# A graph layer on one core: normalised rows and transposed exponentials moved from VectorE to ScalarE

## What is computed

```
xn = layernorm(x)
x  = x + segment_sum(edge_weight * xn[dst], src) + mix(xn)
x  = x + moe(layernorm(x))            # 8 experts, top 2

mix(f):  Q, K, V = f @ W_q + b_q, f @ W_k + b_k, f @ W_v + b_v
         sm  = softmax(K, axis = nodes)
         lam = sm.T @ V                # 256 x 256
         bn  = batchnorm(lam) * gamma + beta
         return Q @ bn
```

## Time and profile before

| | |
|---|---|
| median of 3 runs | 2375.08 us (2373.32 to 2385.05) |
| profiled execution | 2391.07 us, its span 2389.3 us, mean granted clock of TensorE 0.949 |
| PE busy | 2092.6 us, 88% of the span |
| PE weight loads busy | 1786.0 us, 75% |
| DVE busy | 1496.7 us, 63% |
| ACT busy | 1148.2 us, 48% |
| POOL busy | 1420.8 us, 59% |

### The profile page before, as it was taken

The page is one execution under the profiler, slowest core; times in us unless marked ns, Lnnn a source line. Parts: engine busy times, 40 slices in busy tenths (PEclk is TensorE's granted clock), DMA queues, the critical chain, the costliest instruction groups (busy, mean ns, idle before and its releaser), DMA issues. The chain is left out here.

```text
span 2389.3 us, 36271 instructions
## 1 busy us (share of the span) xinstructions
PE 2092.6 (88%) x11864; PEld 1786.0 (75%) x11864; DVE 1496.7 (63%) x2726; ACT 1148.2 (48%) x3466; POOL 1420.8 (59%) x1282
## 2 busy tenths in 40 slices
PE   5798589998999899989998999899999964888885
PEld 3476477987888789878987888789889963666664
DVE  7895387758775777587758775877467766010112
ACT  4520154555456545554565455545566640333332
POOL 1001667667776776677667776776666621666663
PEclk9998899999999999999999999999999986999996
DMA  7523722232233222322232223222233321555666
GB/s 248 164 71 120 246 89 80 84 92 81 77 87 93 79 79 84 91 82 80 84 91 80 80 87 91 78 83 83 86 112 116 116 86 43 180 182 183 209 210 226
DMA packets 157570, 270.85 MB, mean 113 GB/s; under 512 B 28310, under 2 KB 105125, under 8 KB 157385
## 3 DMA queue, kind: packets, MB, share of 16 engines
q0 software_dynamic: 59584, 161.78, 22.7%
q1 hardware_dynamic: 62796, 72.81, 9.3%
q10 hardware_dynamic: 35004, 33.93, 4.8%
HBM read 223.61 MB, written 45.77 MB: 113 GB/s over the span
## 5 line engine op out<-in xcount | busy, mean ns | idle before, releaser
L1154 POOL DMA_INDIRECT edge_G<-xn_scratch,edge_row_i x1029 | 1165.7, 1133 | 488.2 <-issue 262.2
L1254 ACT ACTIVATE edge_weighted<-edge_hots,bins_scale 128x128 f32<-128x128 bf16 x2401 | 738.7, 391 | 52.3 <-DVE edge_row_hots L1311 52.3
L1221 PE MATMUL edge_op<-edge_win,edge_A 128*128 128x256 f32 x2744 | 663.6, 385 | 60.5 <-issue 43.4
L1221 PEld LDWEIGHTS edge_op<-edge_win,edge_A 128*128 128x128 f32 x2744 | 523.7, 192 | 148.6 <-issue 55.3
L1245 ACT COPY edge_A<-edge_ap 128x512 f32<-128x512 f32 x343 | 200.8, 585 | 734.9 <-PE edge_ap L1204 530.2
L1217 PE MATMUL edge_op<-edge_G,edge_weighted 128*128 128x256 f32 x2058 | 511.0, 384 | 25.8 <-DVE all_xn L1324 21.4
L1306 DVE TENSOR_TENSOR edge_hots<-bins_iota128b,bins_recb 128x1024 bf16<-128x1024 bf16 x343 | 237.1, 691 | 367.8 <-PE edge_ap L1204 272.0
L1217 PEld LDWEIGHTS edge_op<-edge_G,edge_weighted 128*128 128x128 f32 x2058 | 364.7, 191 | 71.8 <-DVE all_xn L1324 25.6
L1204 PEld LDWEIGHTS edge_ap<-edge_weighted,edge_row_hots 128*128 128x128 f32 x2744 | 359.1, 194 | 54.0 <-DMA edge_win<-xn_scratch 13.6
L1204 PE MATMUL edge_ap<-edge_weighted,edge_row_hots 128*128 128x128 f32 x2744 | 371.5, 279 | 15.8 <-DMA edge_win<-xn_scratch 13.2
L1311 DVE TENSOR_TENSOR edge_row_hots<-all_iota,bins_recd 128x512 f32<-128x512 f32 x343 | 238.5, 695 | 0.0
(11 more groups left out here) (291 smaller groups left out, 1849.3 us busy)
## 6 DMA issues: line engine op xcount, KB each, us to landing
exp_w1x<-in_w ACTq DMA_DIRECT2D x105, 256.0 KB
edge_G<-xn_scratch,edge_row_i POOLq DMA_INDIRECT x1029
exp_ys<-ys_scratch SPq DMA_DIRECT2D x12, 1024.0 KB
ln_xin<-in_x SPq DMA_DIRECT2D x12, 512.0 KB, 5.7
xn_scratch<-ln_xnb ACTq DMA_DIRECT2D x12, 512.0 KB, 6.8
xnT_scratch<-ln_xT SPq DMA_DIRECT2D x12, 512.0 KB, 7.0
mix_xg<-xn_scratch SPq DMA_DIRECT2D x12, 512.0 KB, 3.9
mix_ek<-xnT_scratch SPq DMA_DIRECT2D x12, 512.0 KB, 4.8
```

Of the source, the lines that this page charges most:

```text
L1154: pool.indirect_dma_start(out=G[:, t % AHEAD, i, :], out_offset=None, in_=xn_dram, in_offset=bass.IndirectOffsetOnAxis(ap=row_i[:, q % 2, ...
L1221: last = nc.tensor.matmul(op[j][:, :], A[:, j, i, :], win[:, q % 2 * DN + i, :], start=False, stop=i == DN - 1)
L1254: last = nc.scalar.activation(weighted[:, t % 2, i, :], hots[:, t % 2, i // 2, :, i % 2], ACT.Copy, scale=scale[:, b, i:i + 1])
```

## The change

Two edits. In the norm stage VectorE normalises one row of tiles of a group and ScalarE the other three. In the mix stage the copy of the transposed exponentials, `evac`, goes from VectorE to ScalarE with its waits: unit 0 between the exponentials of groups 0 and 1, and unit u+1 at the head of ScalarE's step u, in front of the exponentials of a later group and of ScalarE's share of the binning. VectorE keeps its other work in its old order.

```diff
-    DVE_ROWS = 2
+    DVE_ROWS = 1
...
+                def evac(u):
+                    act.wait_ge(p_turned, u + 1)
+                    if u >= PB:
+                        act.wait_ge(p_used, u - PB + 1)
+                    rows = tiles_of(u)
+                    r, w = rows[0], len(rows) * D
+                    nc.scalar.copy(pt[:r, u % PB, 0:w], kp[u % 2][:r, 0:w]).then_inc(p_out, 1)
+
                 exps(0)
+                evac(0)
                 exps(1)
                 for u in range(U):
+                    if u + 1 < U:
+                        evac(u + 1)
                     if u % 2 == 1 and u // 2 + 2 <= NG:
                         exps(u // 2 + 2)
                     for n in IN_SUMS[u]:
...
-                def evac(u):
-                    dve.wait_ge(p_turned, u + 1)
-                    if u >= PB:
-                        dve.wait_ge(p_used, u - PB + 1)
-                    rows = tiles_of(u)
-                    r, w = rows[0], len(rows) * D
-                    nc.vector.tensor_copy(pt[:r, u % PB, 0:w], kp[u % 2][:r, 0:w]).then_inc(p_out, 1)
-
-                evac(0)
                 bins.dve_relate(dve)
                 for u in range(U):
-                    if u + 1 < U:
-                        evac(u + 1)
                     for n in IN_SUMS[u]:
                         bins.dve_share(dve, 0, n)
```

## The result

The changed kernel took 2369.32 us (median of 20 runs, 2363.16 to 2375.15), the kernel before beside it 2374.57 (20 runs, 2368.21 to 2385.05). The ratio is 0.9979, with an interval of 0.9969 to 0.9988: 5 us faster, by its interval 2.9 to 7.4 us. The profiled execution took 2373.04 us, its span 2371.3, against 2391.07 and 2389.3 before. One run in this document, of the cut kernel with the order fixed (297.36 us), was in a slower state of the chip and is left out of its median.

The account below looks back on a forecast made before the run. TensorE, full beside VectorE in the main mix sums (128.2 to 187 us), was taken as the bound there. Norm stage -0.1 and mix sums -0.7 gave -0.8 us: from 2375.08 to 2374.3 us, range 2366 to 2381.

Parts of the forecast that it names:

- The case of a small gain of 0 to 4 us: Whole kernel: the forecast itself, likeliest time 2374.3 us; chance 0.73.
- the step for the copies ahead of the restart: Mix stage: four copies of 0.60 us leave VectorE's queue before the first slot matrix, so TensorE restarts 2.4 us earlier.
- The slow clock: Mix stage: TensorE's longer wait before its restart costs 0 to 1.7 us more at lower clock; 1.7 taken.
- rival (2): Mix sums: VectorE is what really bounds them, so 18 us go, giving 2357 us; chance 0.04.
- Behind the scaled sums: End of mix stage: the chain of dependent steps to 212 us and the last pass run as now.
- the first meeting: Norm stage, group 5: VectorE's shift starts 0.77 us before GpSimd's subtraction, so the 3 us stall goes.
- The two delays of the first groups: Norm stage: by group 5, +0.65 us on VectorE's shift and +1.5 us on ScalarE's cast, hence on GpSimd's subtraction.
- Rival (1): Norm stage: the stall stays, the stage ends 3.0 us later, kernel 2.3 us slower at 2377.4; chance 0.2.
- the term that was mis-sized: Norm stage: one-hot comparisons may meet GpSimd's second subtraction, at most one instruction's wait, inside VectorE's slack.
- part 1: Norm stage: stall gone (-2.05 us) against four longer ScalarE normalisations of 0.49 us each, -0.1 us at its end.
- Busy times: Both early stages: VectorE about 22 us less busy, ScalarE about 22 us more, by mean durations.
- Rival (3): Mix stage: copies queue behind the exponentials on ScalarE, TensorE gives 17 us back, 2391 us; chance 0.03.

Follow-up runs that it names:

- cut kernel with the order fixed: Kernel before, ended behind the mix stage, with GpSimd's two subtractions made to wait for VectorE's rows of groups 5 and 7: 293.09 us.
- third chip: Chip where four whole kernels were run against the kernel before (2241.71 us); the changed kernel took 2238.95 us there, ratio 0.9989.
- cut kernel before: Kernel before without its edge, routing and expert stages, storing x after the mix stage: 298.35 us.
- kernel with the useless matmuls: Changed kernel, ended behind the mix stage, with 44 unused matmuls in TensorE's wait for the first slot matrix: 294.14 us.
- cut kernels with two rows: Two kernels ended behind the mix stage, VectorE keeping two rows: the kernel before (298.35 us) and one with only the copies moved to ScalarE (295.00 us).
- cut pair: Kernel before and changed kernel, both ended behind the mix stage: 298.35 and 294.86 us, difference -3.5 us (-5.6 to -1.7).
- the kernel with the order fixed: Whole kernel before, nothing moved, GpSimd's two subtractions waiting for VectorE's rows of groups 5 and 7: 2238.51 us, ratio 0.9979.
- cut one with only the row: Kernel before, ended behind the mix stage, with one row moved to ScalarE and the copies left on VectorE: 296.19 us against 298.35.

## Why the prediction held, and where it was off

*Sign and size.* Forecast -0.8 us, 2374.3; measured 5.2 us less, 2369.3, inside the range of 2366 to 2381. The case of a small gain of 0 to 4 us was the right one of the four, its size too small. On the third chip the same change gave 2.8 us, with an interval that reaches zero. The range was made wide for the wandering of the medians, so a number inside it says little about the mechanisms; those are gone through one by one.

*Mix stage: the step for the copies ahead of the restart.* Right. 4 x 0.60 = 2.4 us was the term. In VectorE's order of time the start of the slot computation (L398) and the restart lie 22.93 or 22.94 us apart in all five profiles with the copies on VectorE, and 20.55 or 20.56 in all nine with the copies on ScalarE: 2.38 us. The restart came only 1.98 us closer to the stage's start in the whole pair (126.19 - 95.42 against 128.23 - 95.48), because the way from there to the slot computation wanders, from 9.2 to 11.0 us in either group of kernels. The three longest of these stretches have a granted clock of 0.53 to 0.56, the other eleven 0.63 to 0.67. The wait for the slot matrix was put at 6.6 us and is 7.7. The 18 copies behind it brought nothing, as said, and VectorE got its waits for `half_binned` (11.3 us).

*The slow clock.* Put at 1.7 us more than now from the row with 6.48 us of waiting; the rows after give 2.7 - 1.3 = 1.4. The term was near for this pair, and that was in part luck, for two reasons. After one and the same wait of 3.50 us the loss was 0.0, 1.3, 1.5, 1.7 and 2.9 us in five profiles, so taking it from the wait's length does not hold. And before, the loss did not count, because VectorE set the stretch to the scaled sums at 59.9 us and TensorE at full clock needs only 58.2. After, TensorE sets it, at 58.2 plus the whole 2.7. The stretch so became longer by 1.06 us (60.93 against 59.87), not by 1.7 and not by 1.4. So rival (2), VectorE bounds the mix sums, had a part of the truth: VectorE was the bound there, by 1.6 us (59.87 against 58.23) and no more, and taking 14 us from its queue could give no more than that. The time it foretold, 2357, was far off. The scaled sums came 0.98 us earlier; forecast 0.7.

*Behind the scaled sums.* "Run as now" was the claim. From the scaled sums to the last pass lie 24.12 us before and 25.06 after. Nearly all of it comes in the products with `bn` (L879, L882): 4.3 us from the first to the share behind them before (206.24 to 210.54), 5.1 after (205.39 to 210.51). In the profiles of all kernels this stretch is 24.1 to 25.2 us, the cut kernel before among the longest (25.24), so this wanders by itself and is not the change's.

*Norm stage: the first meeting.* Right in the order, with luck in it. Shift ahead of subtraction by 0.77 us was worked out, 0.65 is measured, both about a microsecond earlier than forecast (41.85 and 42.50 against 42.88 and 43.65). The two delays of the first groups were put at +0.65 and +1.5 us and are -0.38 and +0.35; only their difference came near (0.85 and 0.73). Over the eight profiles with one row and no fixed order the lead is 0.08 to 0.79 us. Against the profile of before the stage ended at -0.06 us, forecast -0.1. Rival (1), the stall stays and the stage ends 3.0 us later, needed this order the other way; it occurred once, in a weakened form, in the kernel with the useless matmuls (norm stage at 97.70, about the level of the cut kernel before).

*Norm stage: the term that was mis-sized.* "Other two-input instructions, the one-hot comparisons, may now meet GpSimd's second subtraction; that is at most one instruction's wait, inside VectorE's slack." The comparison did meet it and took 3.21 us for two where one takes 1.02. It was not quite inside the slack: the next shift stood behind it (61.06), and ScalarE's normalisation at 61.26 waited 0.42 us for that. Whether any of this reaches the stage's end is not shown. But the argument looked only for what the change would newly collide. It did not ask what the kernel before would collide in other executions. In the profile that I read, the second subtraction (58.65) came when the last row of the pair (58.08 to 58.82) was under way. In both cut kernels with two rows it hit, for 3.64 and 3.68 us, and the stage ended at 97.9 to 98.1 instead of 95.5. So part 1 was worth not -0.1 but up to -2.8 us (97.86 to 95.02), depending on the execution of before. With -0.9 for the mix part of the whole pair (-2.4 for the copies, +0.4 by the wandering, +1.1 by the clock) this gives -3.8, within the cut pair's -3.5 (-5.6 to -1.7) and within the whole pair's interval. The profiles of the cut pair are further apart than its medians, by 6.3 us at the scaled sums (191.62 against 185.31): -2.8 in the norm stage, -1.7 by the wandering behind it, -2.4 by the copies, +0.6 by the clock. So 1.7 us of what these two profiles differ by is of neither edit. How often the whole kernel before hits at the second meeting is not known, as only one execution of it has a trace; that this is the rest of the 5.2 us is argued from the cut kernels and from the kernel with the order fixed, whose gain of 0.9979 comes from nothing but that order, or from the wait's side effects on the stage.

*Busy times.* VectorE was to lose about 22 us and ScalarE to gain as much: 1496.7 to 1478.1 and 1148.2 to 1168.3, so 18.6 and 20.1. The 22 were by mean durations, in which the overlap of neighbours counts twice; by steps the prediction had 18 for each. The copy on ScalarE is 585 ns by its group after, the normalised row 605, as priced.

```profile
L675 ACT ACTIVATE ln_xnb<-ln_xin,ln_shift,ln_rstd 128x256 f32<-128x256 f32 x36 | 19.1, 605 | 1.2 <-DVE ln_shift L582 1.2
...
L924 ACT COPY mix_pt<-mix_kp 128x512 f32<-128x512 f32 x24 | 14.0, 585 | 46.4 <-PE mix_kp L704 46.4
```

Rival (3), copies late on ScalarE: no wait of TensorE for L924 is in the trace after; ScalarE waits for TensorE instead, 46.4 us. Refuted.

*Open.* The two whole profiles differ by 18 us in the spans, some 12 of them by the end of the edge stage (about 1950 us before, 1938 after), whose code is the same. A part lies at its beginning: at 400 us the kernel after is one step of the edge loop ahead (138 matmuls of L1217 in the trace from 270 us on, against 132, six to a step), 4.6 us. ScalarE in order of time, before and then after:

```profile
302.16 0.58 ACT L1245 COPY edge_A<-edge_ap 128x512 f32<-128x512 f32 x1 [14.60 <-remote]
```

```profile
306.53 0.59 ACT L1245 COPY edge_A<-edge_ap 128x512 f32<-128x512 f32 x1 [8.89 <-remote]
```

ScalarE stands for 14.6 us in one and 8.9 in the other, on something that the profile doesn't name; the DMA engines are 85% busy from 268 to 300 us in both. In the profiles of the third chip this stop is missing. No experiment was made on it, and whether the change has a part in it is open.

## What to carry to other kernels

Where two engines exclude each other for the length of an instruction, and their order is decided by tenths of a microsecond, one profile shows only one outcome: list every pair that comes within a microsecond, price both outcomes, and fix the order with a wait, which here gave as much as the whole change (3.2 and 2.8 us). Where two engines are both full, the shorter one's own length (58.2 against 59.9 us) bounds what relieving the other can give, and a gain of the released work needs the next wait filled: putting TensorE's shares three units later gave 9.8 us on top of the change, on the chip where the change itself gave 2.8. And where profiles of the same code differ by a microsecond or two, measure a term between two landmarks that nothing else comes between: from slot computation to restart the copies were worth 2.38 us in fourteen profiles, while from the stage's start they seemed to be worth anything from 0.9 to 4.2.

## What the runs showed of the hardware

- VectorE's normalisation with two scalars per partition (L589, 128x256, fp32, one tensor input) is blocked by a running GpSimd `tensor_tensor`, whole: 3.34 us instead of 0.41, and 3.64 instead of 0.74. Statistics (L564) beside the same subtraction were not slowed: 1.40 us for four in either case.
- After 3.50 us of waiting TensorE restarted at the lower clock in three kernels (2.03 or 2.02 us for the share: the kernel before, the cut one with only the row, the whole one with the order fixed), at the full one in another (1.18 us, the cut kernel before), and in a fifth it fell to the lower one behind the share (1.28 us, then 3.52 for the sums, which take 1.89 at the full one; cut with the order fixed). Between the same instructions, the same wait cost 0.0, 1.3, 1.5, 1.7 or 2.9 us; waits of 7.36 to 7.68 us cost 1.7 to 2.7.
